# A decoder layer on one core: what stands ahead of the first scan, two gates in free banks, rounding and input norms on ScalarE, the order of queue and queries

## The reference, cut to what matters

```python
x = x + attn_ref(layernorm(x), ...)      # Mamba block, rmsnorm, GELU feed-forward, rmsnorm
x = x + xattn_ref(layernorm(x), ctx_768, ...)
x = x + ffn_ref(layernorm(x), ...)
# Mamba block
u, z = split(x @ in_proj_w.T)            # 512 channels each
u = silu(causal_dwconv(u, conv_w, conv_b))
dt, Bm, Cm = split(u @ x_proj_w.T)       # 16, 16, 16
delta = softplus(dt @ dt_proj_w.T + dt_proj_b)
# for each of 16 states n:  h = exp(delta*A)*h + (delta*u)*B ;  y += h*C
y = (selective_scan(u, delta, A, Bm, Cm) + u*D) * silu(z)
```

## Time and profile before

| what | value |
|---|---|
| three timed runs | 1408.26 us median, 1404.2 to 1411.13 |
| profiled execution | 1410.29 us, its span 1408.5 us |
| busy share of the span | TensorE 90%, ScalarE 67%, VectorE 53%, GpSimd 28% |
| first scan starts | 48.82 us |
| last scan starts | 627.42 us |
| first exponential of the attention starts | 708.57 us |

### The profile page before, as it was taken

How to read it: one execution, slowest core, us unless ns; L and a number is a source line. 1 busy time by engine, 2 the same in 40 slices (tenths; PEclk the granted TensorE clock), 3 DMA queues, 4 the chain that set the end, 5 groups by cost and what they waited for, 6 DMA issues and landing times.

```text
span 1408.5 us, 14664 instructions
## 1 busy us (share of the span) xinstructions
PE 1272.4 (90%) x5502; PEld 622.8 (44%) x5502; DVE 749.1 (53%) x840; ACT 942.6 (67%) x1340; POOL 400.0 (28%) x312
## 2 busy tenths in 40 slices
PE   5669997888988897899789999999999999999999
PEld 2234443434443363355522223223223235588988
DVE  4799989999999999984340000000000138560011
ACT  3867645677647854653399999999999975752300
POOL 1567765566646665750000000000000010000000
PEclk9789989899999998999999999999999999999999
DMA  5433585333323433459260000000000000202601
GB/s 163 152 119 120 174 234 199 110 122 120 120 90 128 136 129 110 149 183 238 70 181 1 1 1 1 1 1 1 1 0 1 1 0 30 78 13 103 286 16 45
DMA packets 43015, 127.73 MB, mean 91 GB/s; under 512 B 6103, under 2 KB 21399, under 8 KB 39544
## 3 DMA queue, kind: packets, MB, share of 16 engines
q1 hardware_dynamic: 42940, 126.75, 28.1%
HBM read 109.64 MB, written 17.09 MB: 90 GB/s over the span
## 4 chain that ended last, share of the span: by engine, by line
PE 57%; DVE 19%; ACT 16%; issue 6%; DMA 1%; POOL 0%; DVEq 0%; SPq 0%; ACTq 0%; POOLq 0%
PE ps L2070 11%; PE ps L2058 10%; DVE ps L1200 9%; ACT arena L1032 7%; PE ps L1857 5%; DVE arena L1211 4%; PE ps L2217 4%; PE ps L2260 4%; PE ps L2141 4%; PE ps L1918 3%; PE ps L1636 3%; ACT ps L806 2%; PE ps L1903 2%; PE ps L2235 2%; PE ps L2248 2%
## 5 line engine op out<-in xcount | busy, mean ns | idle before, releaser
L1032 ACT ACTIVATE arena<-ps,bound 128x1024 f32<-128x1024 f32 (+1 forms) x416 | 425.4, 1120 | 13.8 <-PE ps L2058 5.5
L625 POOL TENSOR_TENSOR arena<-arena 128x1024 f32<-128x1024 f32 x128 | 302.0, 2359 | 222.4 <-DVE arena L1211 168.9
L1200 DVE TENSOR_TENSOR_SCAN ps<-ps,arena 128x1024 f32<-128x1024 f32 x128 | 300.6, 2348 | 13.0 <-ACT ps L806 8.2
L1857 PE MATMUL ps<-arena,ident 128*128 128x512 f32 x512 | 241.7, 618 | 5.1 <-DVE arena L1211 5.1
L2058 PE MATMUL ps<-arena 97*128 97x512 bf16 (+1 forms) x832 | 214.0, 384 | 19.1 <-ACT arena L1032 13.7
L2070 PE MATMUL ps<-arena 128*32 128x512 f32 (+1 forms) x1664 | 207.3, 600 | 0.5 <-ACT arena L1032 0.5
L806 ACT ACTIVATE ps<-arena 128x512 f32<-128x512 f32 x256 | 166.2, 682 | 52.7 <-DVE arena L1211 48.8
L612 POOL TENSOR_TENSOR rstd<-ve,mhalf 128x4 f32<-128x4 f32 (+3 forms) x23 | 25.6, 1113 | 543.1 <-DVE ve L1496 467.0
L1523 DVE COPY arena<-ps 128x512 f32<-128x512 f32 x16 | 11.1, 691 | 288.7 <-PE ps L2070 288.7
L1211 DVE TENSOR_TENSOR arena<-ps,arena 128x1024 f32<-128x1024 f32 x128 | 155.8, 1217 | 10.6 <-DMA arena<-bc_scratch 4.7
L1857 PEld LDWEIGHTS ps<-arena,ident 128*128 128x128 f32 x512 | 99.9, 199 | 131.6 <-issue 120.8
(11 more groups left out here) (194 smaller groups left out, 1370.5 us busy)
## 6 DMA issues: line engine op xcount, KB each, us to landing
arena<-bc_scratch SPq DMA_DIRECT2D x128, 512.0 KB, 4.4
arena<-in_mw SPq DMA_DIRECT2D x16, 1024.0 KB, 9.0
qx_scratch<-arena SPq DMA_DIRECT2D x48, 128.0 KB, 3.1
arena<-qx_scratch SPq DMA_DIRECT2D x4, 1536.0 KB
arena<-kx_scratch SPq DMA_DIRECT2D x1, 4803.0 KB
kx_scratch<-arena SPq DMA_DIRECT2D x36, 128.0 KB, 4.4
arena<-vx_scratch SPq DMA_DIRECT2D x1, 3328.0 KB
vx_scratch<-arena SPq DMA_DIRECT2D x6, 512.0 KB, 2.9
```

The source lines that it names most:

```text
L625: pool.tensor_tensor(dbu[:, w % DR], du[:, DP * p:DP * p + DP], over(bg[:, w // BG % 2, n % BG], DP), ALU.mult).then_inc(S["dbu_ready"], 1)
L1032: act.activation(flat(prob[v % 3][0:n, 2 * h:2 * h + 2]), ps[0:n, 2 * (r % 3):2 * (r % 3) + 2, :].rearrange("p a b -> p (a b)"), ACT.Exp, ...
L1200: dve.tensor_tensor_scan(decay_banks(w), decay_banks(w), flat(dbu[:, w % DR]), carry[:, DP * p, n:n + 1], ALU.mult, ALU.add).then_inc(S["s ...
L1857: last = mm(bank(x), ident[:, :], state(2 * j + s)[:, x], start=False, stop=(j % HP == HP - 1 and (j in SUMMED or s == 1)))
```

## The change

It consists of these parts.

1. **Ahead of the first scan.** VectorE starts with the norm of chunk 0 and prepares its constants later. TensorE starts with 18 matmuls whose result nobody reads (`WARMING`). The gates d = 0 and 1 of chunk 0 are projected right behind the channels into banks 2 and 3, which no scan uses yet, and ScalarE takes them between the channels' silus. ScalarE loads the tables of exp ahead of need with two activations of one column, writes |x| only, and VectorE makes max(x, 0). VectorE itself makes the first scan's input (`first_input`) instead of GpSimd.
2. **Chunk 0 hands nothing on**: the carry is zero there, so L628 and the product in `step_heads` are left out in chunk 0.
3. **Rounding by ScalarE**: 1+e is written by ScalarE (Identity with bias 1.0) behind exp; `step_rounded` is gone, `step_rest` subtracts both in one instruction. The ln moves to a step of its own.
4. **Input norms by ScalarE**: for chunks 1 to 3 VectorE makes only -mean*rstd of 4 columns (`input_shift`) and ScalarE does the four tiles (`normed_input` there), at step 5 of chunk 0 and step 22 of chunks 0 and 1.
5. **Queue order**: the stores of values stand one pair of states later each, and the load of wout and the loads of w1 and w2 are split and stand up to two pairs later.
6. **Query order** ahead of the attention: the squares of chunk 2 go to a buffer of their own and `head_lengths` of them stands behind both projections of chunk 3.

```diff
@@ scalar, one chunk's step size and norm
             def step_exp(c, p):
...
                 act.activation(flat(sp_exp), flat(sp_exp), ACT.Exp, scale=-1.0).then_inc(S["sp_act"], 1)
+                act.wait_ge(S["sp_act"], softplus_steps(h) + 3)
+                act.activation(flat(sp_cor), flat(sp_exp), ACT.Identity, bias=1.0).then_inc(S["sp_act"], 1)
...
+            def normed_input(c):
+                act.wait_ge(S["shift_ready"], c)
+                for i in range(CT):
+                    act.activation(a0[:, c % 3, i], xt[:, c * CT + i, :], ACT.Identity, bias=crec[:, i:i + 1],
+                                   scale=rstd[:, i:i + 1]).then_inc(S["a0_ready"], 1)
@@ scalar, ahead of the first scan
             rank_b_c(0)
-            step_input(0, 0)
+            act.activation(nmx[:, 0:1], half[:, :], ACT.Exp)
+            for x in range(DP):
+                act.wait_ge(S["dt_ps"], x + 1)
+                act.activation(sp_exp[:, x], work(x), ACT.Abs, bias=ch("dt_b")[:, x:x + 1]).then_inc(S["sp_act"], 1)
             step_exp(0, 0)
             step_log(0, 0)
-            head_decays(0, 0)
+            act.activation(nmx[:, 1:2], half[:, :], ACT.Exp)
@@ scalar, the steps
-                    if c == 0 and i < 2:
-                        gate_input(0, 2 * i)
-                        gate_input(0, 2 * i + 1)
+                    if i == 0 and c == 0:
+                        gate_input(0, 2)
+                        gate_input(0, 3)
...
                     if i == 5 + late:
                         step_exp(c, 1)
+                    if i == 6 + late:
                         step_log(c, 1)
...
                     if i == 23 and more:
                         step_exp(c + 1, 0)
+                    if i == (25 if c else 24) and more:
                         step_log(c + 1, 0)
...
+                    if i == 5 and c == 0:
+                        normed_input(1)
+                    if i == 22 and c + 2 < NC:
+                        normed_input(c + 2)
@@ vector
-            def step_rounded(c, p):
-                h = c * DP + p
-                dve.wait_ge(S["sp_act"], h * 5 + 3)
-                dve.tensor_scalar(flat(sp_cor), flat(sp_exp), 1.0, 1.0, ALU.add, ALU.subtract).then_inc(S["sp_step"], 1)
...
+                dve.scalar_tensor_tensor(flat(sp_cor), flat(sp_cor), 1.0, flat(sp_exp), ALU.subtract,
+                                         ALU.subtract).then_inc(S["sp_step"], 1)
...
+            def first_input():
+                dve.wait_ge(b_in[0], 16)
+                dve.wait_ge(S["du_ready"], 1)
+                dve.tensor_tensor(dbu[:, 0], du[:, 0:DP], over(bg[:, 0, 0], DP), ALU.mult).then_inc(S["prep_dve"], 1)
...
                     if i == 20:
-                        normed_input(c + 2)
+                        input_shift(c + 2)
@@ sync
-                if q in (14, 15, 16):
-                    store_values(2 * q - 28)
-                    store_values(2 * q - 27)
-                if q == 17:
+                if q in (15, 16, 17):
+                    store_values(2 * q - 30)
+                    store_values(2 * q - 29)
+                if q == 18:
                     store_values(6)
...
                 if q == 20:
+                    load_wout()
+                if q == 21:
                     store_keys(3, 2)
+                if q == 22:
                     load_ffn()
@@ tensor
+            for n in range(WARMING):
+                mm(bank(5)[:, 0:P], ones[:, :], ident[:, :], start=True, stop=True)
             turn_input(0)
...
-            rank_b_c(0)
+            for d in range(2):
+                project(bank(2 + d), DB + d).then_inc(S["z_ps"], 1)
+            pe.wait_ge(S["u_raw"], DB - 1)
+            for d in range(DB):
+                rank_part(0, d)
             step_input(0, 0)
...
             project_query(2)
-            pe.wait_ge(S["q_act"], q_count(2, "qsq"))
-            head_lengths(ps[0:NH, 1, :], xat[2])
             turn_half(0)
+            pe.wait_ge(S["q_act"], q_count(2, "qf"))
             project_half(0)
             turn_half(1)
+            project_half(1)
+            pe.wait_ge(S["q_act"], q_count(NC - 1, "qsq"))
+            head_lengths(ps[0:NH, 1, :], squares)
             lengths_half(0)
-            project_half(1)
             lengths_half(1)
```

More of the change, by code:

```diff
@@ L1368, in _ @@
             conv_keep(0)
-            step_rounded(0, 0)
+            for x in range(DP):
+                dve.wait_ge(S["sp_act"], x + 1)
+                dve.tensor_scalar(delta[:, x], work(x), ch("dt_b")[:, x:x + 1], 0.0, ALU.add, ALU.max).then_inc(S["sp_in"], 1)
             step_rest(0, 0)
@@ L1952, in _ @@
                         step_input(c, 1)
[L1953 removed]
+                    if i == (5 if c == 1 else 6) and more:
                         turn_input(c + 1)
```

179 lines of the change are left out of this document (101 added, 78 removed).

## The result

| | before | changed |
|---|---|---|
| timed runs | 1408.26 us median of 5 (1404.2 to 1411.45) | 1394.97 us median of 5 (1393.9 to 1397.98) |
| profiled span | 1408.5 us | 1393.0 us |
| first scan | 48.82 us | 39.74 us |
| last scan | 627.42 us | 614.48 us |

The ratio is 0.99, with a 95% interval of 0.9884 to 0.9917: faster by 1%, 13.3 us in the medians and 15.5 in the profiled spans. I had forecast 24.8 and a range of 1369 to 1394. The kernel came out 1 us above its upper end.

The account below looks back on a forecast made before the run. It took VectorE to bound the scans and a chain of engines waiting for each other to bound the start; 12.1 + 2.5 + 3.7 + 2.1 + 2.1 + 2.3 = 24.8 us off median 1408.3 gave 1383.5, stated as 1384, range 1369 to 1394.

Parts of the forecast that it names:

- Start: Ahead of the first scan: 12.1 us less, bounds 6 and 13, with the first scan at 36.7 instead of 48.82.
- steps 1 and 2: Start: norm at about 4.9, 2.2 us less; TensorE at fast pace, convolution starting at 14.4 instead of 18.9.
- Rival C: TensorE stays slow in the start, losing 6 of 12 us: 1390, range 1389 to 1399, chance 0.15.
- Step 3: Start: with two gates projected in the gap, dt, B and C end at 24.9 instead of 33.05, 8.2 us less.
- Step 4: Start: from the evacuation of dt, B and C to the first scan 11.9 us instead of 15.7, 3.9 less.
- What leaves VectorE: Scans: norm tiles 8.1 us and roundings 6.5 leave VectorE, 1.3 comes in: 13.3 us gross.
- Chunk 0: Gain 2.5 us of 7.4, bounds 0 and 10: TensorE stands 4 to 5 us for key lengths, then loses 2.5.
- rival D: TensorE keeps half clock from 166 to the end of chunk 0, 36 us more: 1420, chance 0.03.
- Rival B: ScalarE not late for TensorE in chunk 0, so no new gap: 1376, range 1367 to 1377, chance 0.25.
- Chunk 1: Roundings 1.8, norm 1.2 and the wait for C 1.9 go, 1.2 lost to ScalarE: 3.7 us (1.5 to 4.9).
- Into chunk 2: Decays come 2.6 us earlier; their wait and a rounding of 0.9 go, 0.7 returns: 2.1 us less.
- Ahead of the attention: Last length reduction 7 to 8 us behind the last norm tiles, not 9.6: 2.3 us less (0 to 3).

Follow-up runs that it names:

- heads first: Changed kernel with ScalarE taking the head decays' exp ahead of the copy of a pair of values at step 28 of chunk 0: 1395.55 us.
- first product alone: Changed kernel with GpSimd starting step 1's product only once VectorE is through with the first scan's own product: 1394.92 us.
- three edits (first product not alone): Kernel with four edits less one: GpSimd's first product again starts beside VectorE's: 1382.21 us.
- the lengths early: Changed kernel with ScalarE copying the third group's key lengths at step 24 of chunk 0, ahead of the ln and its table loads: 1388.98 us.
- the sum first: Kernel with four edits, with the eight matmuls adding the states of steps 28 and 29 ahead of the last keys: 1383.57 us.
- "best": Kernel with the sum first, with ScalarE also copying the last key lengths one step earlier, ahead of the key part: 1384.21 us.
- the norm in the hole: Changed kernel with ScalarE's four norm tiles for chunk 2 at step 20 of chunk 0 instead of step 22: 1390.43 us.
- four edits: Changed kernel plus chunk 2's norm tiles at step 20, third-group key-length copy earlier, GpSimd's first product behind VectorE's, chunk 1's norm statistics before the step size: 1383.31 us.

## Why the prediction was wrong

**Start, steps 1 and 2: right.** Norm at 4.81 (4.9), projections at 11.02, convolution at 14.31 (14.4), pace 0.43 from the first, which the run without unread matmuls ties to them. Rival C did not come, though the measured time lies in the range that I gave it (1389 to 1399): that is chance. **Step 3: nearly.** dt, B and C end at 25.34 (24.9). **Step 4: wrong by 2.45.** "and 1.2 for the first scan's input": it took 3.36, because GpSimd starts its own products in the same moment; that is 2.2 of the 2.45. I had seen the same kind of instruction drawn out beside GpSimd in chunk 0 and used its quiet price. The run with the product alone shows the 1.22.

**What leaves VectorE.** The gross saving is to be seen scan by scan: the norm of step 4 gives 2.9 us at the scan of step 5, the two roundings of chunk 1 give 1.5 and its norm 1.1. But up to step 21 of chunk 0 it came to 3.9, not 6.5: VectorE waits 1.34 for TensorE at step 6 and 1.35 for ScalarE at step 8, where I had counted 0.9 in all, 0.41 at step 14, and 1.00 for a row at 137.05, which I had listed as hidden.

**Chunk 0: the steps that failed.** The gap of TensorE came, for the cause and at the instruction named, shorter (2.43 for 4 to 5). Two terms of my 2.5 us were wrong, and together they make the 5.5 us by which it missed.

The first is what came behind the gap. "It came back within 9 us each time with work queued" failed, and with it the "2.5 us behind the new gap". The half clock lasted 13.7, 13.7, 17.1 and 17.1 us in the four traces with this gap (the changed kernel, heads first, first product alone, no unread matmuls), and 6.4 us were lost in the first and not 2.5. The sentence was wrong of the kernel before already. Inside the 39 us that I took as work at full pace, its clock was at half for 10 us, with TensorE busy throughout (all engines; TensorE's columns come first, the clock is the third value from the end):

```profile
196.00:206.00 10.00, 10.00 (x21) 5.00 (x22) 7.63 (x5) 5.45 (x13) 5.78 (x6) 0.50 0.80 227
```

This second stretch was 10.2 us long before and 6.8 in the changed kernel (192.8 to 199.7), which gave 1.7 us back. In all, from the matmul behind the gap (160.53) to the gated product (204.45) it is 43.9 us, where 39.0 became 41.5 in my sum: 2.4 us of the miss.

The second is where this stretch begins. I let VectorE's saving of 6.5 us move it forward by 5.1, from 171.50 to 166.4. It began at 160.53, and with the 9.08 us of the start added that is 169.6: 1.9 us forward and not 5.1. Most of it is VectorE's saving, 3.9 and not 6.5. That is the other 3.2 us of the miss.

It was the mechanism of rival D in part, which had asked for all 39 us at half clock. Rival B, no gap, did not come either. And what the sum leaves out is how little of VectorE's saving can count once TensorE's stretch decides: norms on VectorE, norms on ScalarE, head decays earlier, first scan earlier, all give 1395. What the runs of 1394 to 1396 with the norms on VectorE did is in no trace.

**The other terms** fell within 1 us. Chunk 1's wait for a row of C is gone, as said. Into chunk 2 the decays' wait and the rounding give 2.4 us at step 8 (I had 2.85), but 0.8 is lost at step 3, where the gated product now waits for TensorE, and 0.4 at step 7, where ScalarE's wait grew to 1.28:

```profile
345.58 1.23 DVE L1264 TENSOR_TENSOR arena<-ps,arena 128x1024 f32<-128x1024 f32 x1 [0.71 <-PE ps L1909]
364.62 2.36 DVE L1245 TENSOR_TENSOR_SCAN ps<-ps,arena 128x1024 f32<-128x1024 f32 x1 [1.28 <-ACT ps L832]
```

Ahead of the attention the last reduction comes 6.9 us behind the end of the last norm tiles (677.93 to 684.80), where it was 9.6 and I said 7 to 8.

## What to carry to other kernels

Price a wait that a change puts before TensorE by what the clock does after it, and read the granted clock over the whole stretch that is to be moved before naming a recovery: the longest half clock in it counts, not the one looked at first; a copy of 0.2 us that stood a few instructions too late cost 5 to 6 us here, and 3.65 us of useless matmuls were cheaper than 2.43 of idleness. Before adding up what leaves the busiest engine, ask stage by stage whether a second engine is close behind it (here 138 and 154 of 160 us): there the saving can be worth nothing until that one is relieved too. And look for what an instruction with two operands in memory will run beside: take its price beside GpSimd unless the timeline shows that GpSimd is quiet.

## What the runs showed of the hardware

**Behind gaps of about the same length the half clock lasts from 3 to 17 us.** The gaps of 2 us and more between 140 us and the gated product, and the granted clock of 0.50 behind them, read in windows of 1 us:

| kernel | gap, and its end | half clock | lasts |
|---|---|---|---|
| before | 2.51, 154.15 | 155.1 to 161.9 | 6.8 |
| changed | 2.43, 160.53 | 162.1 to 175.8 | 13.7 |
| heads first | 2.43, 160.91 | 162.5 to 176.2 | 13.7 |
| first product alone | 3.00, 159.16 | 158.9 to 176.0 | 17.1 |
| no unread matmuls | 3.23, 164.08 | 165.0 to 182.0 | 17.1 |
| norms on VectorE | 2.34, 143.56 | 144.8 to 151.6 | 6.8 |
| three edits (first product not alone) | 2.08, 140.69 | 142.5 to 145.9 | 3.4 |

Behind its gap TensorE was busy without a break in each of these stretches. The ends for the changed kernel, heads first and the first product alone lie within 0.4 us of each other for beginnings up to 3.6 us apart. And with the lengths early the clock was at half from 151.1 to 158.0 though TensorE had stood no more than 0.36 us at a time since 128.43. What sets the beginning and the end no run here shows. The Trainium skill (TensorE: Matmul & The Clock Gate, What's actually happening) gives the direction, half clock from idleness. Most traces here agree, and the one with the lengths early does not.

**What a short gap costs depends on more than its length.** 0.48 us at 159.54 left the clock at 1.00, and so did 0.97 us at 128.43 with the lengths early. All twelve traces that have the gap of 0.75 us ahead of the last keys have half clock within 2.8 us behind it, for 3.4 to 10.2 us, and the two in which it is closed (the sum first, and "best") have none there. It came at once in the kernel with the norm in the hole (first row) and later in the one with four edits (second row):

```profile
184.08 1.97 PE L1694 MATMUL ps<-arena 96*128 96x65 f32 x8 [0.75 <-ACT arena L892]
178.31 1.10 PE L1695 MATMUL ps<-arena 96*128 96x65 f32 x8 [0.75 <-ACT arena L894]
```

The same eight matmuls take 1.97 and 1.10 us, and the sixteen of the sum behind them 9.70 and 8.83, where 7.03 is the full pace.

**GpSimd and VectorE slow each other down, at a price that depends on who starts when.** VectorE's product takes 3.36 us when GpSimd starts in the same moment and 1.22 when GpSimd waits; GpSimd's two then take 5.62 us, where one takes 2.34 to 2.36 later in the chunk. The Trainium skill (GPSIMD Engine Reference, Specifications) names contention with instructions of VectorE that have two inputs in SBUF; the trace agrees, with 3.36 us against 1.22.
